# One fused FFN kernel: DVE's and ACT's queues reordered in pairs 0 and 2, x's first tile in three loads, no filler matmuls between products, the last piece's high part mixed first

## What is computed

```python
h = gelu(cond @ W0 + b0); h = gelu(h @ W1 + b1)
att = softmax(h @ W2 + b2)                       # 64 samples x 8
agg_w = einsum('bk,koi->boi', att, weight)       # a 64 x 64 mixing matrix per sample
y = einsum('boi,bih->boh', agg_w, x) + (att @ bias_k)[:, :, None]
scores = y @ gate_w.T + gate_b                   # 4 experts of ranks 8, 16, 32, 64
lora = y @ A[:r].T @ B[:, :r].T                  # r: the rank of the best score
out = x + (y @ W.T + b) + lora
```

## Time and profile before

| | us |
|---|---|
| median of three executions | 458.8 |
| profiled execution, its time | 458.18 |
| profiled execution, span | 456.3 |
| TensorE busy (matmul) | 450.4 |
| VectorE (DVE) busy | 343.8 |
| ScalarE (ACT) busy | 181.4 |
| GpSimd (POOL) busy | 19.4 |

### The profile page before, as it was taken

One profiled execution on the slowest core, in us unless ns is written; L12 is line 12 of the kernel. 1 busy time (PEld: TensorE's weight loads), 2 busy tenths in 40 slices (PEclk: granted clock), 3 DMA queues, 4 the chain that ended last, 5 costly groups with the idle time before them and its releaser, 6 DMA issues.

```text
span 456.3 us, 10477 instructions
## 1 busy us (share of the span) xinstructions
PE 450.4 (99%) x3510; PEld 445.8 (98%) x3510; DVE 343.8 (75%) x889; ACT 181.4 (40%) x415; POOL 19.4 (4%) x46
## 2 busy tenths in 40 slices
PE   9999999899999999999999999999999999999997
PEld 7999999899999999999999999999999999999997
DVE  4887988799586876958687695868769586876945
ACT  5654554455243343524334342433334243342511
POOL 1010000010000000000000000000000000100000
PEclk9999999999999999999999999999999999999999
DMA  7973560711608053250805235080523408052202
GB/s 273 344 277 54 145 227 1 239 46 52 232 1 278 6 188 97 88 195 0 281 1 194 88 90 192 0 278 4 201 81 108 174 5 277 0 190 95 92 2 93
DMA packets 23773, 59.18 MB, mean 130 GB/s; under 512 B 6862, under 2 KB 8834, under 8 KB 23684
## 3 DMA queue, kind: packets, MB, share of 16 engines
q1 hardware_dynamic: 23508, 58.78, 39.0%
q10 hardware_dynamic: 240, 0.07, 0.1%
HBM read 40.69 MB, written 18.15 MB: 129 GB/s over the span
## 4 chain that ended last, share of the span: by engine, by line
PE 96%; DVE 3%; ACT 1%; issue 0%; POOL 0%; ACTq 0%; POOLq 0%
PE p_p L1071 74%; PE p_o L1089 4%; PE p_o L1091 4%; PE p_o L1109 3%; PE p_o L1090 3%; PE p_o L1108 3%; PE p_p L1115 1%; PE p_p L1136 1%; PE p_p L1097 1%; PE p_o L1136 1%; DVE wl L716 1%; DVE w_raw L722 1%; DVE zl L792 0%; DVE aggw L776 0%; DVE prod L773 0%
## 5 line engine op out<-in xcount | busy, mean ns | idle before, releaser
L1071 PE MATMUL p_p<-wh,xh 128*128 128x274 f32 (+1 forms) x880 | 256.6, 292 | 0.0
L1071 PE MATMUL p_p<-wh,xl 128*128 128x274 f32 (+1 forms) x880 | 254.2, 289 | 0.0
L1071 PE MATMUL p_p<-wl,xh 128*128 128x272 f32 (+1 forms) x864 | 250.5, 290 | 0.0
L1071 PEld LDWEIGHTS p_p<-wh,xh 128*128 128x128 f32 x880 | 166.5, 189 | 0.4 <-issue 0.4
L1071 PEld LDWEIGHTS p_p<-wh,xl 128*128 128x128 f32 x880 | 166.7, 189 | 0.1
L1071 PEld LDWEIGHTS p_p<-wl,xh 128*128 128x128 f32 x864 | 163.0, 189 | 0.1
L579 ACT ACTIVATE zh<-sv 128x274 fp32r<-128x274 f32 (+1 forms) x56 | 24.3, 433 | 95.0 <-DVE sv L804 95.0
L811 DVE TENSOR_TENSOR xin<-p_o,xin 128x274 f32<-128x274 f32 (+2 forms) x128 | 52.0, 418 | 2.7 <-PE p_o L1109 1.9
L557 ACT ACTIVATE xh<-s_raw 128x512 fp32r<-128x512 f32 x60 | 36.3, 628 | 17.1 <-DVE s_raw L759 16.4
L579 ACT ACTIVATE zh<-p_p 128x272 fp32r<-128x272 f32 (+1 forms) x44 | 17.5, 398 | 60.7 <-PE p_p L1071 59.0
L766 DVE TENSOR_TENSOR xl<-s_raw,xh 128x512 fp32r<-128x512 f32 x60 | 40.9, 682 | 0.1
(11 more groups left out here) (140 smaller groups left out, 508.4 us busy)
## 6 DMA issues: line engine op xcount, KB each, us to landing
xin<-in_x SPq DMA_DIRECT2D x32, 512.0 KB, 4.0
raw<-in_xt SPq DMA_DIRECT2D x31, 512.0 KB, 5.2
out<-xin SPq DMA_DIRECT2D x30, 512.0 KB, 5.9
w_raw<-in_w SPq DMA_DIRECT2D x8, 274.0 KB, 7.0
w_raw<-in_w SPq DMA_DIRECT2D x8, 272.0 KB, 6.0
g_aggw<-aggw_all SPq DMA_DIRECT2D x8, 128.0 KB, 2.4
aggw<-g_aggw SPq DMA_DIRECT2D x15, 64.0 KB, 5.0
out<-xin SPq DMA_DIRECT2D x4, 137.0 KB, 2.1
```

Source lines behind the costliest of these rows:

```text
L1071: last = nc.tensor.matmul(o[:, 0:W[r]], a, m, start=start and p == 0, stop=stop and p == 2, skip_group_check=True)
```

## The change

Six edits. On SP, the 768 columns of x's first tile are loaded in two DMAs, 256 columns behind W's piece 0 and 512 columns behind piece 1, with a semaphore of their own for the first. On ACT, w_hi(10) and w_hi(11) move ahead of bd_hi and the high part of b. On DVE in pair 0, the copies `att_rows` and `attt` move behind A22's low part and w_lo(5), w_lo(8) moves ahead of cs_lo(1), and w_lo(9) behind Z12's low part. On DVE in pair 2, the first T-sum goes ahead of the second bd_lo and Z11's low part goes ahead of a residual and the second T-sum. On TensorE, the fillers of `first_unit` go. And the last piece of the last pair (Z21) is no longer made by `mix` and `lora`: its four matmuls that need only the high part are issued first, then the wait for the low part and its one matmul.

```diff
@@ sync
             for m, (r, n, h) in enumerate(W_ORDER):
                 sp.dma_start(w_raw[r][:, RAW_OF[n], 2 * h:2 * h + 2, :], w_in[r][m % 8 // 2, h]).then_inc(s_w_in[m], 16)
                 if m == 0:
-                    sp.dma_start(raw[:, 0, FIRST * P:], xt[0][:, FIRST * P:]).then_inc(s_raw_in[0], 16)
+                    sp.dma_start(raw[:, 0, FIRST * P:HB], xt[0][:, FIRST * P:HB]).then_inc(s_raw_rest_in, 16)
+                if m == 1:
+                    sp.dma_start(raw[:, 0, HB:], xt[0][:, HB:]).then_inc(s_raw_in[0], 16)
@@ scalar
             z_hi(0, 0, 0, Z11)
+            w_hi(10)
+            w_hi(11)
             act.wait_ge(s_clear, 5)
             bd_hi(0, 0, 0)
             bd_hi(0, 0, 1)
             act.wait_ge(s_brow_in, 16)
             nc.scalar.activation(b_h.bitcast(F32R), b_raw, ACT.Copy).then_inc(s_b_hi, 1)
-            w_hi(10)
-            w_hi(11)
             cs_hi(1)
@@ vector, pair 0
-            dve.wait_ge(s_raw_in[0], 16)
+            dve.wait_ge(s_raw_rest_in, 16)
             rest = slice(FIRST * P, HB)
             nc.vector.tensor_copy(xh[:, A11, rest], raw[:, 0, rest]).then_inc(s_x0h, 1)
...
             w_lo(1)
+            dve.wait_ge(s_raw_in[0], 16)
             nc.vector.tensor_copy(xh[:, A12, :], raw[:, 0, HB:H]).then_inc(s_x0h, 1)
...
                 w_lo(3 + n)
-                if n == 1:
+                if n == 2:
                     dve.wait_ge(s_rows_mm, 1)
...
             nc.vector.tensor_copy(kern_h[:, :], kern_s[:, :]).then_inc(s_kern_hl, 1)
+            w_lo(8)
             cs_lo(1)
             z_lo(0, 0, 0, Z22)
...
-            w_lo(8)
+            z_lo(0, 0, 0, Z12)
             w_lo(9)
-            z_lo(0, 0, 0, Z12)
             w_lo(10)
             z_lo(0, 0, 0, Z21)
@@ vector, step
+                if two:
+                    t_sum(0, R11, R12, R11)
                 bd_lo(i, j, 1)
+                if two:
+                    z_lo(i, j, 0, Z11)
                 if not one:
                     residual(i, j - 1, 1, Z21)
                 if two:
-                    t_sum(0, R11, R12, R11)
                     t_sum(0, R12, R22, R12)
                 elif not one:
                     s_lo(i, j, S3)
-                z_lo(i, j, 0, Z11)
+                if not two:
+                    z_lo(i, j, 0, Z11)
@@ tensor, first_unit
                     if kk % 2 == 0:
-                        if at < 2:
-                            keep_busy(2)
                         pe.wait_ge(s_wl, at + 1)
@@ tensor, end
-            for n in (Z12, Z21):
-                mix(*last, 1, n)
-                lora(*last, 1, n)
+            mix(*last, 1, Z12)
+            lora(*last, 1, Z12)
+
+            cols, mine = COLS[1][Z21], slice(P, 2 * P)
+            o, zs = p_o[:, OBANK[Z21], 0:W[1]], slice(0, W[1])
+            pe.wait_ge(s_zh, piece(*last, 1, Z21))
+            pe.wait_ge(s_y, piece(*last, 1, Z21 - 4))
+            nc.tensor.matmul(o, bd[:, 1, 0, :], zh[:, 1, zs], start=True, stop=False)
+            nc.tensor.matmul(o, bd[:, 1, 1, :], zh[:, 1, zs], start=False, stop=False)
+            nc.tensor.matmul(o, ut_hl[:, mine], bt_h[:, cols], start=False, stop=False)
+            nc.tensor.matmul(o, ut_h1[0:ROWS, mine], bt_l[0:ROWS, cols], start=False, stop=False)
+            pe.wait_ge(s_zl, piece(*last, 1, Z21))
+            nc.tensor.matmul(o, bd[:, 1, 0, :], zl[:, 1, zs], start=False, stop=True).then_inc(s_lora, 1)
```

More of the change, by code:

```diff
@@ L221, in adaln_ffn @@
         s_raw_first_in = sem("s_raw_first_in")
+        s_raw_rest_in = sem("s_raw_rest_in")
         s_stored = [sem(f"s_stored{i}") for i in range(4)]
```

## The result

| | before | changed |
|---|---|---|
| median, 22 executions each | 458.53 us | 460.97 us (457.79 to 463.19) |
| ratio to the kernel before, 95% interval | 1 | 1.0037 (1.0020 to 1.0054) |
| profiled execution, time | 458.18 | 461.85 |
| profiled execution, span | 456.3 | 458.6 |

What follows compares the result with a forecast made beforehand. TensorE, busy for all but 5.9 us of the span, was taken as the bound. Start 0.5, pair 2 1.5 and end 0.5 sum to 2.5 us off the 458.8 median: 456.3, range 454.9 to 457.6.

Steps and rivals of the forecast that it cites:

- Pair 2's stall: TensorE's wait at Z11's mix in pair 2 goes, DVE's low part coming earlier: 1.5 us, bounds 1.1 and 1.5.
- The end: Last piece: four matmuls needing only the high part start before the low part is ready: 0.5 us, bounds 0.25 and 0.6.
- The start's terms: Fillers, DMA order, DVE and ACT moves, Z12's stall: TensorE 1.65 us ahead at 28.16, of which 0.5 us is kept.
- What is late next: Mixing products: k_rows land as before, TensorE waits 1.1 us and starts at 41.9; start keeps 0.5 us, bounds 0 and 1.65.
- x in three DMAs: Start: W's second piece lands about 0.6 us earlier; the third DMA itself costs nothing, bounds 0 and 0.2.
- rival C: Start: without fillers TensorE's clock rises later; slower only if over 7.2 us late, 462.7 at 15 us; chance 0.03.
- A: Mixing products: k_rows are not the limit, so the start keeps 1.65 us, 3.65 in all: 455.1; chance 0.12.
- D: Pair 2: the edits don't remove the wait, ACT's high part or bd_hi becoming the releaser: 457.8; chance 0.05.
- B: More is swallowed: the start keeps nothing, or pair 2 gives 1.1 us: 456.8 to 457.2; chance 0.27.
- the stall at the hook: Sign that more of the gain is swallowed: a TensorE stall there of over 0.3 us.

Runs made afterwards that it cites:

- e12: Kernel before with only SP's order mended (kernels' split stored earlier, k_rows loads moved ahead, x for residuals behind them): 458.42 us, ratio 0.9997.
- e8: Changed kernel with the attention copies ahead of A22's low part again, as before: 460.92 us, ratio 1.0017.
- e7: Changed kernel with the two filler pairs between the first products again: 460.08 us, ratio 0.9994.
- e3: Changed kernel with 12 filler matmuls of 512 columns issued where TensorE waits for k_rows: 458.26 us, ratio 0.9993.
- f4: Kernel before with SP's order mended, pair 2 and last-piece edits, the w_lo(8), w_lo(9) order, and no fillers: 455.06 us, ratio 0.9924.
- e5: Changed kernel with SP's order mended (kernels' split stored earlier, k_rows loads moved ahead, x for residuals behind them): 456.28 us, ratio 0.9939.
- e1: Kernel before with only the late edits (pair 2 and the last piece): 457.39 us, ratio 0.9969.
- e10: Kernel before without the fillers between the first products, nothing else changed: 458.80 us, ratio 1.0002.
- e4: Changed kernel with x's first tile in two loads again: 458.71 us, ratio 1.0.
- f2: Changed kernel, unchanged, run for a second profile: 463.51 us.
- e2: Changed kernel with SP storing the kernels' split before the gate-rows wait and k_rows loads ahead of the second column-sum rows: 457.62 us, ratio 0.996.

## Why the prediction was wrong

**Pair 2's stall** was right: TensorE's mix of Z11 follows the matmul before it by 0.13 (88.84, 88.97), and between pair 1's and pair 2's first mixes 1.42 us are gone (29.54 before, 28.12 after), besides the restart. DVE's queue did what the step said: two T-sum halves went into its idle time (it now waits 0.39 for ACT before Z11's low part, which is done 1.1 us before TensorE wants it).

**The end** was right for TensorE, 0.5 of the 0.63 us being its own and 0.1 pair 2's restart; but from the last matmul's start to the end of the span it is now 3.29 us instead of 2.99, so 0.3 comes off where I had only said that the stores lie closer. That is no chance of one profile: it is 2.96 to 3.04 in the five profiles with the old end and 3.17 to 3.56 in the thirteen with the new one. Both late terms together are 1.42 + 0.63 - 0.3 = 1.75 instead of 2.0 us.

**The start's terms** were too good. I had TensorE 1.65 us ahead at Z12's mix; it was 28.16 - 26.88 = 1.28 ahead in the profile, after 0.5 us for W's third piece and 0.7 for `attt` (0.2 forecast). ACT's high part of W's second piece came early, as forecast (6.82; near 7.2 was said). W's third piece I had not looked at: with x's half behind piece 1, piece 2 comes later, and ACT starts its high part at 9.13 instead of 8.78:

```profile
8.78 0.64 ACT L520 ACTIVATE wh<-w_raw 128x544 fp32r<-128x544 f32 x1
```

```profile
9.13 0.66 ACT L523 ACTIVATE wh<-w_raw 128x544 fp32r<-128x544 f32 x1 [1.38 <-DMA w_raw<-in_w]
```

The clock also rose sooner than in the profile of before: matmuls of 272 columns follow each other by 0.13 from 6.68 on, in the profile of before only from 9.77 on. That is not the change's doing. In e12, whose first products are those of before, they do so from 6.47 on, and in e8, which has no fillers, only from 10.29 on.

**The step that failed** is "What is late next", in the sentence "No edit touches bytes ahead of that, so k_rows land when they did". The bytes were the same and the landing was not: SP gets past g_rows 1.43 us later (28.15 against 26.72), and across 18 profiles by 1.4 with x in three loads. So TensorE waited 2.4 us (4.2 in the second profile), not 1.1. In the sum's own terms: it arrived at 43.59 - 2.37 = 41.22 instead of 40.8, and k_rows were there for a start at 43.59 instead of 41.9. By the estimate above k_rows land near 42.1 even with SP's times of before, so the landing was read well for the old kernel, and the term would have been some 0.3 instead of 0.5; what was wrong is that it stays. In "x in three DMAs" the third load was priced at 0, bounds 0 and 0.2, for what stands in front of TensorE directly; the queue behind it was not priced at all. The fixed cost that the prediction takes from the Trainium skill there is given, in the anatomy section of "DMA: Bandwidth & Descriptors", for DMAs that GpSimd issues; these are SP's, and no run here shows it.

**The second half of the failure** is rival C. I tied the falling clock to the missing fillers and let the k_rows wait hide the loss. It is the k_rows wait itself that the clock falls behind in the changed kernel: with the fillers back it still falls (e7, 9 of 12), with the wait filled it mostly doesn't (e3, 2 of 12), and without fillers and without the wait it stays up (f4, 0 of 8; e5, 1 of 10). Its price in the trace: 6.8 us at half the level, 2.9 us of delay. With the 1.1 us by which the mixing product itself was late, that is the 4.05 us which outweighs 1.42 + 0.63. That the wait for k_rows would appear was forecast; that a wait can cost about as much again behind it was not.

Rivals A and D fell: k_rows were the limit, and pair 2's wait went. Two signs of B came, the mixing products at 43.59 ("42.4 or later") and the stall at the hook of 0.7 us ("over 0.3"); its direction was right and its size, a start that keeps nothing, was not.

## What to carry to other kernels

An engine that arrives early at a transfer does not merely lose its lead: if TensorE then stands still, its clock can fall and the wait is paid for about twice (2.37 us of wait and 2.93 us of slow matmuls behind it here). So before stalls are taken out of the front of a kernel, move the transfer that is next in line (here SP's order: small stores that something depends on ahead of bulk loads that nothing needs yet), or fill the wait. Do not price a load that is cut in two by its bytes alone; look at when the transfers that depend on that queue get through, in several profiles: two profiles of the same kernel lay 0.3 us (before) and 1.1 us (changed) apart at g_rows.

## What the runs showed of the hardware

The clock did not fall after every wait, and the length of the wait does not say when. It stayed up after 1.56 us idle (e1) and fell after 1.46 (e10), 2.30 (e8), 2.37 (changed), 3.3 (e4), 4.2 (f2) and 4.7 us (e7); in e2 it fell behind a wait of 0.7 us, and in e5 it stayed up behind one of 0.6. The slow stretch does not follow the length either: it lasted 3.4 us in e2, e4 and e10, 6.8 in the changed kernel, e7 and f2, and 10.2 in e8. In each of these profiles the clock fell for one stretch and rose again while TensorE was busy. One profile each can't say how often a wait of a given length ends so.

The time at which the queue let g_rows go varied by 2.0 us among the kernels with x in two loads (26.42 to 28.46) and by 1.9 among those with three (27.64 to 29.58). Some of that can be the kernels' other edits; between the two profiles of the changed kernel it was 1.1 us (28.15 and 29.28).
